# Moving one of the five time-mix additions from GpSimd to VectorE

## What is computed

```python
sx  = shift(x) - x
mix = tanh((x + sx * x_maa) @ tm_w1)          # five groups of 32 columns
mw, mk, mv, mr, mg = per_group(mix @ tm_w2)
wx = x + sx * (w_maa + mw)                    # f = 0, feeds the decay
kx = x + sx * (k_maa + mk)                    # f = 1
vx = x + sx * (v_maa + mv)                    # f = 2
rx = x + sx * (r_maa + mr)                    # f = 3
gx = x + sx * (g_maa + mg)                    # f = 4
w  = tanh(wx @ td_w1) @ td_w2;  k = kx @ Wk;  r = sigmoid(rx @ Wr);  v = vx @ Wv
```

## Time and profile before

| | |
|---|---|
| median of 3 runs | 2960.12 us |
| the profiled execution's own time | 2952.02 us |
| its span | 2950.2 us |
| TensorE matmul busy (PE) | 2746.5 us, 93% |
| VectorE busy (DVE) | 2425.3 us, 82% |
| ScalarE busy (ACT) | 1382.7 us, 47% |
| GpSimd busy (POOL) | 1305.0 us, 44% |
| GpSimd additions L770 | 320, 402.0 us, mean 1273 ns |
| VectorE products L1117 | 640, 270.1 us, mean 475 ns |

### The profile page before, as it was taken

The page is one execution under the profiler, slowest core; times in us unless marked ns, Lnnn a source line. Parts: engine busy times, 40 slices in busy tenths (PEclk is TensorE's granted clock), DMA queues, the critical chain, the costliest instruction groups (busy, mean ns, idle before and its releaser), DMA issues.

```text
span 2950.2 us, 82824 instructions
## 1 busy us (share of the span) xinstructions
PE 2746.5 (93%) x34621; PEld 2186.3 (74%) x34621; DVE 2425.3 (82%) x5345; ACT 1382.7 (47%) x2899; POOL 1305.0 (44%) x1457
## 2 busy tenths in 40 slices
PE   4778999999999999999999999999999999999875
PEld 3567877777787777778777777777777777777753
DVE  5657888888888888888888888888888888888754
ACT  2435455554445455444555544445555444455331
POOL 3344444444444455444445544444554544444310
PEclk8889999999999999999999999999999999999987
DMA  4000000000000000000000000000000000000000
GB/s 152 15 5 9 13 9 9 9 12 13 12 13 13 5 9 13 13 12 13 13 5 9 12 13 13 13 13 5 12 9 12 13 13 13 5 9 12 9 8 7
DMA packets 36849, 41.77 MB, mean 14 GB/s; under 512 B 3272, under 2 KB 35200, under 8 KB 36480
## 3 DMA queue, kind: packets, MB, share of 16 engines
q1 hardware_dynamic: 35696, 36.32, 3.8%
q10 hardware_dynamic: 784, 0.16, 0.0%
HBM read 28.08 MB, written 8.39 MB: 12 GB/s over the span
## 4 chain that ended last, share of the span: by engine, by line
PE 67%; DVE 19%; ACT 6%; issue 5%; POOL 2%; ACTq 0%; DVEq 0%; DMA 0%; POOLq 0%
PE ps_all L1529 11%; PE ps_all L1515 9%; PE ps_all L1548 8%; PE ps_all L1324 8%; PE ps_all L1566 5%; PE ps_all L1316 5%; PE ps_all L1354 3%; PE ps_all L1427 3%; DVE mixin L1117 3%; PE ps_all L1308 2%; DVE att L1167 2%; PE ps_all L1340 2%; PE ps_all L1422 2%; DVE sxrk L1135 2%; PE ps_all L1485 2%
## 5 line engine op out<-in xcount | busy, mean ns | idle before, releaser
L770 POOL TENSOR_TENSOR mixin<-mixin,hT_tm 128x512 f32<-128x512 f32 x320 | 402.0, 1273 | 357.4 <-DVE mixin L1117 357.4
L1515 PE MATMUL ps_all<-chan,cwk 128*128 128x256 f32 x1536 | 386.4, 395 | 12.2 <-DVE chan L1096 9.6
L1529 PE MATMUL ps_all<-cwv,chan 128*128 128x256 f32 x1536 | 350.0, 384 | 0.0
L1515 PEld LDWEIGHTS ps_all<-chan,cwk 128*128 128x128 f32 x1536 | 280.4, 192 | 76.7 <-issue 33.6
L1529 PEld LDWEIGHTS ps_all<-cwv,chan 128*128 128x128 f32 x1536 | 288.0, 191 | 48.6 <-issue 9.3
L750 POOL TENSOR_TENSOR rstd<-var,powc 128x2 f32<-128x2 f32 x224 | 179.2, 800 | 308.3 <-DVE var L1056 307.7
L911 ACT ACTIVATE chan<-ps_all 128x512 f32<-128x512 f32 x192 | 114.7, 598 | 422.0 <-PE ps_all L1515 420.0
L1117 DVE SCALAR_TENSOR_TENSOR mixin<-ps_all,vcol,sxrk 128x256 f32<-128x256 f32 x640 | 270.1, 475 | 22.2 <-PE ps_all L1354 12.6
L1167 DVE COPY_PREDICATED att<-masks,ps_all 128x256 f32<-128x256 uint8 x384 | 204.3, 532 | 20.4
L936 ACT ACTIVATE mixin<-ps_all,vcol 128x256 f32<-128x256 f32 x128 | 65.3, 560 | 287.4 <-PE ps_all L1496 287.2
L1548 PE MATMUL ps_all<-gateT,ffn_work 128*128 128x352 f32 x512 | 182.4, 479 | 6.1 <-ACT ffn_work L870 4.5
(11 more groups left out here) (191 smaller groups left out, 6621.6 us busy)
## 6 DMA issues: line engine op xcount, KB each, us to landing
xin<-in_L_attn_x_dram SPq DMA_DIRECT2D x32, 256.0 KB, 2.7
tok<-in_L_attn_x_dram SPq DMA_DIRECT2D x32, 256.0 KB, 2.7
out_dram<-x SPq DMA_DIRECT2D x32, 256.0 KB, 2.1
cwk<-in_L_attn_cWk_dram SPq DMA_DIRECT2D x2, 768.0 KB, 8.0
cwv<-in_L_attn_cWv_dram SPq DMA_DIRECT2D x2, 768.0 KB, 10.0
ffn_work<-in_L_wmod_dram SPq DMA_DIRECT2D x2, 512.0 KB, 4.9
tok<-in_L_ffn_w_down_dram SPq DMA_DIRECT2D x1, 704.0 KB, 4.3
tok<-in_L_ffn_w_gate_dram SPq DMA_DIRECT2D x1, 640.0 KB, 8.4
```

The lines of the kernel that those rows point to most:

```text
L770: pool.tensor_tensor(m, m, hT["tm", l][:, :, :, 1:P + 1].rearrange("p k c t -> p (k c) t"), ALU.add).then_inc(ev["mixed"][b], 1)
L1515: ins = pe.matmul(bank(b, "ck", lj, "k")[:, m * TT:(m + 1) * TT], cwk[:, l, k, n:n + P], k_in[:, k, :], start=(k == 0), stop=(k == KC - 1))
L1529: ins = pe.matmul(bank(b, "cv", l, "v")[:, c * D:(c + 1) * D], relu[t // 2][:, t % 2, c * P:(c + 1) * P], cwv[:, l, t, :], start=(t == 0), ...
```

## The change

VectorE itself adds `hT_tm` to mixed input 0: behind its two products it waits on the bank's `free` semaphore, which its second product increments, and then issues one `tensor_tensor` of 128x512. That instruction increments a new event `mixed_w`, which `pw1` now waits for. The event `mixed` keeps counting the other four. GpSimd's lists lose `mf.0` everywhere; the lists of the other engines are as before. There are 64 such additions, 32 tiles in two layers. The diff, with the lists cut to one line (all the others lose `mf.0` in the same way):

```diff
-    POOL: """2/2 cmix; 0/1 lna.in lna.tm; 4/5 dn; 4/4 lna.out; 0/1 mix; 1/3 st.1; 4/4 lna.ffn; 1/3 gnb; 0/1 mf.0 mf.1 mf.3; 1/3 yt;
+    POOL: """2/2 cmix; 0/1 lna.in lna.tm; 4/5 dn; 4/4 lna.out; 0/1 mix; 1/3 st.1; 4/4 lna.ffn; 1/3 gnb; 0/1 mf.1 mf.3; 1/3 yt; 2/2
...
-    "carried": (["turn"], 1), "shifted": (["mix", "cmix"], 1), "xxx": (["mix"], 1), "tanh": (["mix"], 1), "mixed": (["mf"], 1),
+    "carried": (["turn"], 1), "shifted": (["mix", "cmix"], 1), "xxx": (["mix"], 1), "tanh": (["mix"], 1), "mixed": (["mf"], 1), "mixed_w": (["mf"], 1),
...
-                if kind in kinds:
+                if kind in kinds and (name not in ("mixed", "mixed_w") or (arg[1] == 0) == (name == "mixed_w")):
...
                 ins.then_inc(free_of(b, *(("pw2", l, "w") if f == 4 else ("mf", lf, "m"))), 1)
+                if f == 0:
+                    emptied(v, i, b, "mf", lf, "m")
+                    m = mixes(b, f).rearrange("p k (c t) -> p (k c) t", t=P)
+                    v.tensor_tensor(m, m, hT["tm", l][:, :, :, 1:P + 1].rearrange("p k c t -> p (k c) t"), ALU.add).then_inc(ev["mixed_w"][b], 1)
...
                 fill(pe, i, b, "pw1", l, "d")
-                after(pe, i, "mixed", b, "mf", (l, 0))
+                after(pe, i, "mixed_w", b, "mf", (l, 0))
```

More of the change, by code:

```diff
@@ L42 @@
         3/3 ck.1; 1/2 pk; 4/4 qa.0; 0/1 sc.2; 1/2 pr; 0/1 pg; 1/2 pw2; 0/1 sc.3; 4/4 ht.0""",
-    POOL: """2/2 cmix; 0/1 lna.in lna.tm; 4/5 dn; 4/4 lna.out; 0/1 mix; 1/3 st.1; 4/4 lna.ffn; 1/3 gnb; 0/1 mf.0 mf.1 mf.3; 1/3 yt;
-        2/2 cv; 0/1 mf.2; 1/2 lna.tm; 3/3 lna.cm; 1/2 mix; 3/3 cmix; 0/1 mf.4 tot; 1/2 mf.0 mf.1 mf.3 mf.2 mf.4; 0/1 st.0; 1/2
+    POOL: """2/2 cmix; 0/1 lna.in lna.tm; 4/5 dn; 4/4 lna.out; 0/1 mix; 1/3 st.1; 4/4 lna.ffn; 1/3 gnb; 0/1 mf.1 mf.3; 1/3 yt; 2/2
+        cv; 0/1 mf.2; 1/2 lna.tm; 3/3 lna.cm; 1/2 mix; 3/3 cmix; 0/1 mf.4 tot; 1/2 mf.1 mf.3 mf.2 mf.4; 0/1 st.0; 1/2
         tot; 0/1 st.1; 1/2 st.0; 0/1 gnb yt; 3/3 cv; 2/1 lna.cm""",
@@ L87 @@
         ck.1; 2/1 pk pr; 0/4 ht.0; 3/0 sc.3; 2/1 pw2""",
[L88 to L95, removed]
+    POOL: """0/0 lna.in lna.tm mix mf.1 mf.3 mf.2 mf.4 tot st.0 st.1 gnb yt; 0/2 lna.cm; 1/0 lna.in; 0/2 cmix; 1/0 lna.tm mix mf.1
+        mf.3; 0/2 cv; 1/0 mf.2; 0/1 lna.tm mix; 1/0 mf.4 tot; 0/1 mf.1 mf.3; 1/0 st.0; 0/1 mf.2; 1/0 st.1; 0/1 mf.4;
+        1/0 gnb; 0/1 tot; 1/0 yt; 1/2 lna.cm; 2/0 lna.in; 1/2 cmix; 2/0 lna.tm; 0/1 st.0; 2/0 mix; 0/1 st.1 gnb; 2/0
+        mf.1 mf.3; 1/2 cv; 0/1 yt; 1/1 lna.tm; 0/3 lna.cm; 2/0 mf.2; 1/1 mix; 0/3 cmix; 2/0 mf.4 tot; 1/1 mf.1 mf.3
+        mf.2; 2/0 st.0 st.1; 1/1 mf.4; 2/0 gnb; 1/1 tot; 2/0 yt; 0/3 cv; 1/1 st.0; 2/2 lna.cm cmix; 3/0 lna.in lna.tm;
+        0/4 lna.out; 3/0 mix; 1/1 st.1 gnb; 0/4 lna.ffn; 3/0 mf.1 mf.3; 1/1 yt; 2/2 cv; 3/0 mf.2; 1/3 lna.cm; 2/1
+        lna.tm mix; 1/3 cmix; 3/0 mf.4 tot; 2/1 mf.1 mf.3 mf.2; 3/0 st.0; 2/1 mf.4 tot; 3/0 st.1 gnb; 2/1 st.0; 3/0
+        yt; 1/3 cv; 3/2 lna.cm""",
 }
@@ L177 @@
         gu.0.0 gu.0.1 qa.0 ht.0 gu.1.0 gu.1.1 qa.1 ht.1""",
[L178 to L190, removed]
@@ new lines @@
+    POOL: """-5/2 cmix; -4/0 lna.in lna.tm; -8/4 dn; -4/0 mix; -7/4 lna.out lna.ffn; -6/1 st.1 gnb; -4/0 mf.1 mf.3; -6/1 yt; -4/0
+        mf.2; -5/2 cv; -6/3 lna.cm; -5/1 lna.tm mix; -6/3 cmix; -4/0 mf.4 tot; -5/1 mf.1 mf.3 mf.2 mf.4; -4/0 st.0;
+        -5/1 tot; -4/0 st.1 gnb yt; -6/3 cv; -4/2 lna.cm; -3/0 lna.in; -4/2 cmix; -3/0 lna.tm; -7/4 dn; -3/0 mix; -6/4
+        lna.out lna.ffn; -5/1 st.0 st.1 gnb; -3/0 mf.1 mf.3; -5/1 yt; -4/2 cv; -3/0 mf.2; -4/1 lna.tm; -5/3 lna.cm;
+        -4/1 mix; -5/3 cmix; -3/0 mf.4 tot; -4/1 mf.1 mf.3 mf.2 mf.4 tot; -3/0 st.0 st.1; -4/1 st.0; -3/0 gnb yt; -5/3
+        cv; -3/2 lna.cm; -2/0 lna.in; -3/2 cmix; -2/0 lna.tm; -6/4 dn; -2/0 mix; -5/4 lna.out lna.ffn; -4/1 st.1 gnb;
+        -2/0 mf.1 mf.3; -4/1 yt; -3/2 cv; -2/0 mf.2; -3/1 lna.tm; -4/3 lna.cm; -3/1 mix; -4/3 cmix; -2/0 mf.4 tot;
+        -3/1 mf.1 mf.3 mf.2 mf.4; -2/0 st.0; -3/1 tot st.0; -2/0 st.1 gnb yt; -4/3 cv; -2/2 lna.cm cmix; -1/0 lna.in
+        lna.tm; -5/4 dn; -1/0 mix; -4/4 lna.out; -3/1 st.1 gnb; -4/4 lna.ffn; -1/0 mf.1 mf.3; -3/1 yt; -1/0 mf.2; -2/2
+        cv; -3/3 lna.cm; -2/1 lna.tm mix; -3/3 cmix; -1/0 mf.4 tot; -2/1 mf.1 mf.3 mf.2 mf.4; -1/0 st.0; -2/1 tot;
+        -1/0 st.1 gnb yt; -3/3 cv; -2/1 st.0; -1/2 lna.cm cmix; -4/4 dn; -3/4 lna.out; -2/1 st.1 gnb; -3/4 lna.ffn;
+        -2/1 yt; -1/2 cv; -2/3 lna.cm; -1/1 lna.tm mix; -2/3 cmix; -1/1 mf.1 mf.3 mf.2 mf.4 tot st.0; -2/3 cv; -3/4
+        dn; -2/4 lna.out; -1/1 st.1; -2/4 lna.ffn; -1/1 gnb yt; -1/3 lna.cm cmix cv; -2/4 dn; -1/4 lna.out lna.ffn dn""",
```

## The result

The changed kernel takes 2966.46 us (median of ten runs, 2963.33 to 2971.78) against 2960.01 us for the kernel before (ten runs, 2951.92 to 2963.03): a ratio of 1.0027, 95% interval 1.0017 to 1.0037, so it is slower by about a quarter of a per cent. (The ratio is estimated from all the runs and is not quite that of the medians, 1.0022.) The profiled execution took 2967.97 us, its span is 2966.2 us.

A forecast was written before the change was run, and what follows sets the result against it. TensorE sets the pace, with VectorE's chain from mf.0 to cq.2 setting lev.3. 24.6 x 0.30 = 7.4 us, layer 0 nothing, ends +3 us: +10.4, so 2960.1 becomes 2970.5 us; range 2960 to 2990 us.

The forecast's parts named there:

- the forecast case: Whole kernel: +10.4 us, median 2960.1 becomes 2970.5 us, own range 2966 to 2976; chance 0.50.
- The addition's price: VectorE, behind mf.0's products: addition of 0.69 us, mf.1 follows 1.51 us in instead of 0.79, +0.72 us.
- What comes back in layer 1: L1135 behind mf.1, no longer held by GpSimd's mf.0 addition: 0.42 of 0.72 us returns, leaving +0.30 us.
- Layer 0 costs nothing: Layer 0 on VectorE: the 0.72 us is paid from 1.20 us lost at L585 and L587 waiting for GpSimd.
- The gain at pw1 is waited away: TensorE, layer 1: the 0.35 us gained at pw1 is lost at lev.3, whose wait grows to 0.8 to 0.9 us.
- The size: Repeated order, 430 to 2530 us: 24.6 tiles, each 0.30 us longer, 7.4 us.
- The term for the ends: Ends of the run, 15 of the 64 additions: 0.2 us a place, +3 us.
- A: Rival: no time comes back; layer 1 costs 0.72 and layer 0 0.46 us a tile, 2994 us; chance 0.10.
- B: Rival: layer 0's addition is held by GpSimd's power L794; 16 us more, 2987 us; chance 0.08.
- C: Rival: faster, TensorE keeps its 0.35 us from pw1; 2951.5 us; chance 0.08.
- D: Rival: no measurable change, layer 1 costs 0.2 us or less and the ends hide theirs; 2960 to 2966 us; chance 0.24.
- four waits of TensorE that come once in each tile: TensorE, 430 to 2530 us: waits of 8.1, 6.9, 5.9 and 5.5 us, total 26.4 us, 1.1 us a tile.

The follow-up runs named there:

- The late spare addition: The whole change, but GpSimd keeps a same-size addition in mf.0's place that waits until VectorE's is done: 2970.04 us against 2957.20, ratio 1.0050.
- the last two kernels: Kernel before with VectorE's pg behind cq.2, 2967.15 us; then that plus pw1 behind ck.1 on TensorE and ScalarE, 2981.17 us; both against 2957.20.
- pw1 late: Kernel before with only layer 1's pw1 put behind ck.1 on TensorE and ScalarE: 2970.51 us against 2957.20, ratio 1.0050.

## Why the prediction came out as it did

**The result.** 2966.46 us lies in the range of 2960 to 2990, at the lower edge of the forecast case's own range of 2966 to 2976; the sign is right. The difference of the medians is 6.45 us where 10.4 was said; the ratio makes it 8.0 us, with an interval of 5.0 to 11.0.

**The addition's price.** mf.1 follows 1.52 us behind the first product where 1.51 was said, and the addition takes 0.69 us. Confirmed.

**What comes back in layer 1.** The first L1139 takes 0.68 us, and mf.3 is 0.29 us late where 0.30 was said. The late spare addition shows the cause itself: a GpSimd addition at that time lengthens this instruction again, to 0.96 us. The rule of the Trainium skill, SBUF — State Buffer, "Who interferes with whom", on which that step drew, agrees with these additions: whichever of the two starts first is not lengthened. The one held up ends 0.55 to 0.58 us behind the other, which is less than its own 0.69. For the power in layer 0 the rule does not hold, as the prediction had read from the trace.

**Layer 0 costs nothing.** Shown by itself: 85.44 us with the addition in layer 0 alone. VectorE is 0.23 us ahead at L592 (0.22 was said), and the gain is swallowed by the wait for L1246, the one that the prediction named.

**The gain at pw1 is waited away.** The wait is gone and lev.3 starts 0.30 us later, as said. The form was off in two ways. lev.3's wait did not grow to 0.8 to 0.9 us but to 0.34, because ht.0, two stages ahead of it, also waits for the delayed VectorE, 0.39 us; the prediction looked only at the last of TensorE's readers. And the two together are 0.73 us, less than it said, because TensorE keeps only 0.26 us of pw1's 0.35: ck.1 can't start before ScalarE's L911 is done. Neither changes the end, which VectorE's chain sets.

**The size.** An undisturbed tile became 0.34 us longer where 0.30 was said: 24.6 x 0.34 = 8.4 us instead of 7.4. The term for the ends, +3 us from a guess of 0.2 us a place, is not borne out and not measured either. The medians leave 6.45 - 8.4 = -2 us for it, the ratio and its interval -0.4 us (-3.4 to 2.6). The kernel with layer 1 alone has a difference of medians of 10.1 us against 24.6 x 0.32 = 7.9 us in its tiles, which leaves +2. From nothing it can't be told.

The profiled executions fit if like is put beside like. The kernel with the addition in layer 0 alone has the tile of the kernel before and a span of 2958.2 us, and the changed kernel's 2966.2 is 8.0 us above it. Layer 1 alone, 2960.1 us, is 9.9 us above the 2950.2 of the kernel before. The changed kernel's span is 16.0 us above that last one, but some 7 us of this have nothing to do with the change: they arise before the repeated order has settled, in executions with a lower granted clock. The last section returns to it.

**Rivals.** A (no time comes back, a tile 1.18 us longer) and B (the power holds the addition) are out by the timelines: L1139 took 0.68 us, and the addition 0.69 us inside the power. C (faster) is out: TensorE kept nothing at lev.3. D (2960 to 2966 us, no measurable change) was near: the result lies 0.5 us above its edge, and the interval of the ratio begins at 1.0017. The whole time hardly decides against it; the tile's 0.34 us, where D supposed 0.2 at most, does.

**What the prediction had wrong without harm.** It counted four waits of TensorE that come once in each tile and left out the largest, for the chan of L1072, 13.2 us in 24 times in the kernel before. It is 13.4 us after, so nothing hung on it. It called the tiles copies of one another, and nearly half of them are longer, by up to 1 us; this is so before and after, and the mean moved as the undisturbed tile did. And it took lev.3 to be set by VectorE's chain alone. The second chain, through lev.2, is as tight; an estimate of a change that shortens VectorE's chain would have failed on it, as the expectations for the last two kernels did.

## What to carry to other kernels

An operation that moves to the engine on which others wait costs its length less whatever it takes off that engine elsewhere, here 0.72 - 0.42 us in one layer and 0.72 - 0.95 us in the other, where VectorE came out 0.23 us ahead; look for instructions that take longer than the rest of their group and ask which neighbour's end they share. A wait that a change removes is worth only as much as the next wait behind it leaves, and that next wait may hang on two chains that meet within 0.05 us: then shortening one brings next to nothing (0.05 us here), and lengthening either costs in full. Work that stands in the shadow of another engine's result, as pg did in the kernel before, is free where it is; moved behind the next reader its 0.60 us cost 0.33 us of a tile. In the changed kernel, where VectorE came later than TensorE, the same move gained 0.24 us: what an order is worth depends on which chain is the later one.

## What the runs showed of the hardware

**Who is held up depends on who is first by hundredths.** Of VectorE's and GpSimd's additions 0.04 us apart, VectorE's took 0.69 us and GpSimd's 1.54; with GpSimd's ahead by 0.63 us, GpSimd's took 1.04 and VectorE's 0.96. A VectorE instruction with one of its two tensors in PSUM (L1208, 0.68 us at 1574.23) ran at full speed beside GpSimd's additions of 1573.61 to 1575.93, while a 128x32 instruction with one small input, L585, took 0.43 us beside them (0.19 us in layer 1).

**GpSimd's small powers did not hold VectorE.** The addition in layer 0 started 0.73 us into a power of a 128x8 tile (1.64 us) and took 0.69 us, as it does alone.

**The clock in the first 200 us differs between executions.** The granted clock of TensorE is the number behind the five busy times, here from 20 to 40 us and from 120 to 140 us, for the kernel before:

```profile
20.00:40.00 20.00, 13.75 (x68) 7.44 (x69) 6.56 (x18) 1.88 (x6) 5.21 (x5) 0.74 0.80 253
...
120.00:140.00 20.00, 16.89 (x202) 13.40 (x199) 10.83 (x24) 12.73 (x29) 12.44 (x16) 1.00 0.00 1
```

and for the changed kernel:

```profile
20.00:40.00 20.00, 12.53 (x52) 6.84 (x53) 7.81 (x21) 1.60 (x5) 4.07 (x4) 0.60 0.80 252
...
120.00:140.00 20.00, 17.35 (x137) 12.94 (x139) 8.90 (x23) 9.93 (x24) 9.91 (x13) 0.88 0.00 1
```

From 430 to 2530 us it is 1.00 in both. From 0 to 430 us it is 0.90 in the kernel before and 0.88 in the changed one, and the sixth pw1 of layer 1 starts at 473.1 and at 478.6 us. That this is the execution and not the change is seen in the other profiles: with layer 1 alone the clock is 0.91 and that pw1 starts at 473.8 us, and with pw1 late, where no addition is moved, the clock is 0.88 and it starts at 481.3 us.

The time goes with the clock in the timed runs as well. Of the 38 runs of the kernel before that stand beside the experiments, the 12 with a mean granted clock of 0.976 or more took 2951.8 to 2957.6 us (median 2953.3), and the 10 with 0.973 or less 2957.2 to 2964.3 us (median 2960.8). What makes the clock differ from one execution to the next stays open.
